# TensorE's column tiles take fourths of the tokens, and VectorE's block transposes lay attention output and sums into rows

## The chip, the cores and the metric

One core of one Trainium2 chip runs the whole program: TensorE (matmuls), VectorE, ScalarE, GpSimd, and SyncE (SP), which issues all DMAs. The metric is the device time of one execution in microseconds (us). Before the change it is 1421.83 us, the median of 3 runs (1418.3 to 1422.57).

## What is computed

Two conditioned attention layers on x (8 batches, 512 tokens, 512 channels). Layer 0 is linear attention with 8 heads; layer 1, the one that the change touches, is full softmax attention with 16 heads of 32 channels. Cut to what matters of layer 1:

```python
xn = layer_norm(x, norm_w, norm_b)
q = (xn @ q_w + q_b).reshape(8, 512, 16, 32)          # k alike
att = jnp.einsum('bnhl,bmhl->bnmh', q, k)             # + mask
att = jax.nn.softmax(att, axis=2)
v = ((xn @ v_w + v_b) * src_mask[:, :, None]).reshape(8, 512, 16, 32)
y = jnp.einsum('bnmh,bmhl->bnhl', att, v).reshape(8, 512, 512)
scale, shift = jnp.split((silu(emb) @ emb_w + emb_b)[:, None, :], 2, axis=2)
h = layer_norm(y, sb_norm_w, sb_norm_b) * (1.0 + scale) + shift
return x + silu(h) @ out_w + out_b
```

## The kernel before

Every float32 matrix product but two is made from rounded high parts and remainders, three matmuls a product (`product`, L508 to L510). Tokens come in four tiles of 128 (`NT`), channels in four of 128.

Layer 1's attention runs in 32 units n (`N1`), each one batch b and one group g of four heads, n = 4b + g. Of one unit, by steps of `the_order`:

- `qk`: queries and keys of two units ahead; SP stores them to DRAM (L1535, L1536) and loads them back as the stacks `Qs`, `Ks` (`stack`, L1548), once the current unit's `a` matmuls are done with the buffer.
- `S` (L665): scores of the next unit with tokens on partitions, 16 matmuls; VectorE takes each one's maximum (L1213). `nxt` (L673, L913) brings the negated maxima into rows of `Qs`.
- `a` (L682): the scores again, keys on partitions, with the maximum subtracted, 16 matmuls; ScalarE takes the exponential into `Pb` (L930).
- `pv` (L720), in two parts of two key tiles: values times exponentials into the bank PV. The four heads j of the group take the four column tiles of TensorE (32 output partitions each), and every product streams 512 tokens: PV is [head j and its 32 channels, 512 tokens].
- GpSimd adds the exponentials over the four key tiles (L1376; in the last unit VectorE too, L1242), and `den` (L698) sums them over partitions into the bank DEN with the selecting columns `sel`. It is queued ahead of the next unit's first `pv` part; after a batch's fourth unit it stands in `tlx`.
- `ae` (L938): ScalarE copies PV to `yt`; `tl`: TensorE makes four transposes of `yt` back into PV (helper `turn`, L503), ScalarE copies these to `yb` (L946), tokens on partitions; the semaphore `y1` then frees PV for the next unit.
- once a batch, `tlx`: ScalarE copies DEN to `yt` (L951), four transposes, VectorE takes the reciprocals `rd` (L1259), VectorE and GpSimd multiply `yb` (L1266, L1392). Then `ny` (layer norm, L1052 to L1060, L772), `ty` (transpose, scale, silu; GpSimd makes the remainder `sTl` and counts it in `s_lo`; its first step has SP load the residual rows into the four `wr`, L1497) and `o` (output product, L1199 and stores L1503), beside the units of the next batch.

The order on each engine is one list written out ahead: `weave` merges tracks of steps, and each track has start and end times in `PLAN`, as fractions of a unit (one entry for each g), between which its steps are spread by their `COST`. A unit's track may run past 1, and then ends the unit. Every engine, SP too, takes its own part of the list in order, and semaphores do the rest. PV and DEN are fixed banks; the other six go round.

Of the kernel before, what the change touches and what calls it, by code (L numbers as in the profile page):

```python
# [12 lines left out]
NT = T // 128  # L13
# [21 lines left out]
    "tl": (0.2, 0.1, 0.9), "tlx": (1.0, 0.0, 0.4, 0.4, 0.4, 0.4),  # L35
# [9 lines left out]
    "0q": ((0.109, 0.988), (0, 0.247), (0.978, 1.13)),  # L45
    "0o": ((0.012, 0.84), (0, 0.907), (0.06, 0.131)),
    "att": ((0.155, 0.254, 0.365, 0.543, 0.682), (0.002, 0.187, 0.345, 0.514, 0.66), (0.071, 0.271, 0.519, 0.672, 0.873), (0.001, 0.263, 0.332, 0.52, 0.685)),
    "pv": ((0.365, 0.753, 0.853), (0.337, 0.76, 0.879), (0.489, 1.021, 1.054), (0.328, 0.759, 0.832)),
    "tl": (None, (0, 0.931), (0, 0.654), (0, 0.723)),
    "tlx": ((0.007, 0.493), None, None, None),  # L50
    "ty": ((0, 0.666, 0.76), (0, 0.852, 0.94), (0, 0.862, 0.982), (0, 0.903, 1.096), (0, 0.953, 1.106)),
    "S": ((0.405, 0.476, 0.494, 0.654, 0.71), (0.151, 0.322, 0.491, 0.662, 0.834), (0.186, 0.267, 0.505, 0.626, 0.665), (0.211, 0.35, 0.409, 0.511, 0.65)),
    "nxt": ((0.847, 0.986), (0.899, 0.993), (0.866, 0.886), (0.724, 0.88)),
    "q": ((0.283, 0.391, 0.41), (0, 0, 0.02), (0, 0.151, 0.275), (0, 0.128, 0.394)),
    "k": ((0.337, 0.495, 0.596), (0, 0, 0.02), (0.187, 0.289, 0.357), (0.029, 0.298, 0.304)),
    "stack": ((0.802, 0.802), (0.489, 0.489), (0.812, 0.812), (0.683, 0.683)),
# [202 lines left out]
def cond_two_layers(nc, A, out):  # L259
# [4 lines left out]
    with ctx:  # L264
# [23 lines left out]
        yt = vt[1]  # L288
# [12 lines left out]
        rd = cU[:].rearrange("p a b -> p (a b)").rearrange("p (t g j) -> p t g j", t=NT, g=NG)  # L301
# [6 lines left out]
        sel = sb("sel", [128, 36])  # L308
# [37 lines left out]
        for i in range(2):  # L346
# [22 lines left out]
            "yT", "y1_tr", "y1", "den", "dT", "d1_tr", "rd", "y1_sc")}  # L369
# [124 lines left out]
        def _(e):  # L494
# [190 lines left out]
            def den(i, n):  # L685
                b, g = divmod(n, NG)
                pool, dve = ps_count(n, 3, 3)
                e.wait_ge(s["Ps_pool"], pool)
                if dve:
                    e.wait_ge(s["Ps_dve"], dve)  # L690
                if n == 0:
                    e.wait_ge(s["sel"], 2)
                    if bank_before["bank", 7] is not None:
                        e.wait_ge(*done(bank_before["bank", 7]))
                elif g == 0:
                    e.wait_ge(s["rd"], b)
                for j in range(4):
                    r = e.matmul(DEN[32 * j:32 * j + 32, :], sel[:, 4 - g:36 - g], p_buf(n, 0)[:, j, :],  # L698
                                 start=(g == 0), stop=(g == NG - 1))
                r.then_inc(s["den"], 1)  # L700

            def pv(i, n, first):

                b, g = divmod(n, NG)
                if first == 0 and g:
                    den(0, n - 1)
                for m in (first, first + 1):
                    e.wait_ge(s["P"], 16 * n + 4 * m + 4)
# [13 lines left out]
                    r.then_inc(s["PV"], 1)  # L722

            def tl(i, n):
                b, g = divmod(n, NG)
                if i == 1:
                    e.wait_ge(s["yT"], n + 1)
                    turn(PV, [yt[:, t * 128:(t + 1) * 128] for t in range(NT)]).then_inc(s["y1_tr"], 1)

            def tlx(i, b):  # L730
                if i == 1:
                    e.wait_ge(s["dT"], b + 1)
                    turn(DEN, [yt[:, t * 128:(t + 1) * 128] for t in range(NT)]).then_inc(s["d1_tr"], 1)

            parts = {"m": m, "mb": mb, "tx": tx, "k": k, "v": v, "te": te, "q": q, "st": state, "y": y, "ty": ty, "o": o,
                     "qk": qk, "S": S, "nxt": nxt, "a": a, "pv": pv, "den": den, "tl": tl, "tlx": tlx}
# [5 lines left out]
        def _(e):  # L742
# [189 lines left out]
            def ae(i, n):  # L932
                if n:
                    e.wait_ge(s["y1_tr"], n)
                if n and n % NG == 0:
                    e.wait_ge(s["d1_tr"], n // NG)
                e.wait_ge(s["PV"], 4 * n + 4)
                e.copy(yt[:], PV[:]).then_inc(s["yT"], 1)  # L938

            def tl(i, n):  # L940
                if i == 2:
                    b, g = divmod(n, NG)
                    if g == 0:
                        e.wait_ge(s["s_lo"], 4 * (8 + b))
                    e.wait_ge(s["y1_tr"], n + 1)
                    e.copy(yb[:, :, g * 128:(g + 1) * 128], t4(PV)).then_inc(s["y1"], 1)  # L946

            def tlx(i, b):
                if i == 0:
# [10 lines left out]
        def _(e):  # L960
# [290 lines left out]

            def tlx(i, b):
                if i == 1:
                    if b:
                        e.wait_ge(s["y1_sc"], 4 * b)
                    else:
                        e.wait_ge(s["y_sc"], 64)
                    e.wait_ge(s["d1_tr"], b + 1)
                    e.reciprocal(rd.rearrange("p t g j -> p t j g"),  # L1259
                                 DEN[:].rearrange("p (t j l) -> p t j l", t=NT, j=4)[:, :, :, 0:4]).then_inc(s["rd"], 1)  # L1260
                if i in (2, 4):
                    t = i - 2
# [3 lines left out]
                    e.tensor_tensor(y3, y3, rd[:, t, :, :].rearrange("p g j -> p (g j)").unsqueeze(2).to_broadcast([128, H1, 32]),  # L1266
                                    ALU.mult).then_inc(s["y1_sc"], 1)
# [3 lines left out]
                     "y": y, "ty": ty, "o": o, "qk": qk, "S": S, "nxt": nxt, "a": a, "ae": ae, "tlx": tlx}  # L1271
# [5 lines left out]
        def _(e):  # L1277
            def prologue():
# [10 lines left out]
                e.memset(sel[:, 4:5], 1.0).then_inc(s["sel"], 1)  # L1289
# [112 lines left out]
        def _(e):  # L1402
# [86 lines left out]
            def ty(i, x, c):  # L1489
                if i == 0 and c == 0:  # L1490
# [126 lines left out]
```

## Time and profile before

| | before |
|---|---|
| median of 3 runs | 1421.83 us |
| profiled execution | 1421.4 us |
| its span, first to last instruction | 1419.6 us |
| TensorE busy | 1345.7 us (95%) |
| VectorE busy | 1005.0 us (71%) |
| ScalarE busy | 821.8 us (58%) |
| GpSimd busy | 770.8 us (54%) |
| mean granted TensorE clock | 0.988 of full |

Layer 1's attention takes the span from about 545 us to 1385 us. In the rows, PE is TensorE's matmuls, PEld its weight loads, DVE VectorE, ACT ScalarE, POOL GpSimd, SPq the SP queue that issues DMAs. A matmul's duration is from its issue to its end, with the pipeline in it: matmuls that follow one another overlap. One float32 product with both operands unrounded shows as two matmuls. Some matmul records are missing from a trace.

### The profile page before, as it was taken

To read this page: it belongs to the slowest core of one execution; us is meant where nothing else is said; L and a number is where in the kernel's file an instruction comes from. 1 tells how busy PE (TensorE), PEld (TensorE's weight loads), DVE (VectorE), ACT (ScalarE), POOL (GpSimd) and SP (SyncE) were. 2 spreads that over 40 slices of the span, in tenths; PEclk is the share of its full clock that TensorE was granted. 3 is DMA by queue.
4 is the path that set the end of the run, shared out by engine and by line. 5 is a ranking of instruction groups with operands and counts; after the bars stand their busy time and mean duration, and the time that the engine had idled before them with its cause. 6 is when DMAs were issued, how large, how long until landed. Compare 5 with 4: busy or idle time off the path is not lost.

```text
span 1419.6 us, 20550 instructions
## 1 busy us (share of the span) xinstructions
PE 1345.7 (95%) x7040; PEld 971.0 (68%) x7040; DVE 1005.0 (71%) x1966; ACT 821.8 (58%) x1429; POOL 770.8 (54%) x692
## 2 busy tenths in 40 slices
PE   6899999999999899999999999999999999999887
PEld 4678888888888786566666665666666666666445
DVE  5788978778788876677657657657757756756645
ACT  4255455454554644756756756756756766666663
POOL 0323243332433515467657757757847847846863
PEclk9899999999999999999999999999999999999999
DMA  9021111311213275745545535534634634633602
GB/s 336 1 67 53 46 60 38 97 60 38 68 37 111 91 216 172 221 135 161 143 132 160 156 119 163 165 119 145 182 120 139 182 104 142 200 105 112 180 14 82
DMA packets 82888, 172.93 MB, mean 122 GB/s; under 512 B 7240, under 2 KB 7240, under 8 KB 82784
## 3 DMA queue, kind: packets, MB, share of 16 engines
q1 hardware_dynamic: 82784, 171.62, 39.3%
q8 instruction: 56, 0.92, 0.3%
q14 instruction: 48, 0.39, 0.1%
HBM read 104.45 MB, written 67.14 MB: 121 GB/s over the span
## 4 chain that ended last, share of the span: by engine, by line
PE 65%; DVE 14%; DMA 7%; ACT 6%; issue 3%; POOL 3%; SPq 1%; DVEq 0%; POOLq 0%; ACTq 0%
PE ps L508 13%; PE ps L510 12%; PE ps L509 12%; PE ps L665 6%; PE ps L720 6%; PE ps L682 6%; DVE cT L1213 5%; PE ps L503 4%; DMA Ks<-stack_scratch 4%; PE ps L698 2%; DVE st L1052 2%; POOL yb L1392 2%; PE ps L596 1%; PE ps L617 1%; ACT xTh L786 1%
## 5 line engine op out<-in xcount | busy, mean ns | idle before, releaser
L1376 POOL TENSOR_TENSOR Pb<-Pb 128x512 f32<-128x512 f32 x376 | 470.2, 1289 | 218.4 <-PE ps L720 218.2
L1213 DVE TENSOR_REDUCE cT<-ps 128x1 f32<-128x512 f32 x512 | 326.2, 685 | 131.1 <-PE ps L665 126.3
L930 ACT ACTIVATE Pb<-ps 128x512 f32<-128x512 f32 x512 | 285.9, 602 | 190.3 <-PE ps L682 184.2
L665 PE MATMUL ps<-Ks,Qs 98*128 98x512 f32 x512 | 194.9, 419 | 10.9 <-DMA Ks<-stack_scratch 8.3
L682 PE MATMUL ps<-Qs,Ks 106*128 106x512 f32 x512 | 199.2, 415 | 2.3 <-ACT Qs L913 1.4
L665 PEld LDWEIGHTS ps<-Ks,Qs 98*128 98x128 f32 x512 | 95.4, 191 | 70.9 <-DVE cT L1213 21.4
L682 PEld LDWEIGHTS ps<-Qs,Ks 106*128 106x128 f32 x512 | 95.2, 190 | 50.7 <-issue 25.4
L1299 POOL TENSOR_TENSOR rs<-ve,mhalf 128x4 f32<-128x4 f32 x32 | 33.0, 1032 | 167.8 <-DVE ve L1038 115.3
L1327 POOL TENSOR_TENSOR vt<-vt,qmx 128x512 f32<-128x512 f32 x32 | 33.7, 1055 | 166.1 <-DVE qmx L1130 166.1
L508 PE MATMUL ps<-xTh,Wh_k 128*128 128x512 f32 x256 | 106.5, 416 | 3.6 <-DVE xTl L1065 2.3
L508 PE MATMUL ps<-Wh_o,sTh 128*128 128x512 f32 x256 | 106.3, 415 | 0.2 <-DVE sTl L1191 0.2
L508 PE MATMUL ps<-Wh_v,xTh 128*128 128x512 f32 x256 | 102.9, 402 | 0.0
L510 PE MATMUL ps<-Wh_o,sTl 128*128 128x512 f32 x256 | 101.1, 395 | 0.0
L510 PE MATMUL ps<-Wh_v,xTl 128*128 128x512 f32 x256 | 100.7, 394 | 0.0
L510 PE MATMUL ps<-xTh,Wl_k 128*128 128x512 f32 x256 | 100.7, 393 | 0.0
L509 PE MATMUL ps<-Wl_o,sTh 128*128 128x512 f32 x256 | 100.6, 393 | 0.0
L509 PE MATMUL ps<-xTl,Wh_k 128*128 128x512 f32 x256 | 100.2, 391 | 0.0
L509 PE MATMUL ps<-Wl_v,xTh 128*128 128x512 f32 x256 | 100.2, 391 | 0.0
L1340 POOL TENSOR_TENSOR wr<-wr,boB 128x512 f32<-128x512 f32 x64 | 83.5, 1320 | 15.7 <-DMA wr<-in_x 13.7
L1199 DVE TENSOR_TENSOR wr<-ps,wr 128x512 f32<-128x512 f32 x64 | 43.8, 688 | 43.9 <-PE ps L510 31.8
L1113 DVE TENSOR_TENSOR ps<-ps,bvB 128x512 f32<-128x512 f32 x64 | 44.5, 697 | 40.5 <-PE ps L510 39.8
L1065 DVE TENSOR_TENSOR xTl<-ps,xTh 128x512 fp32r<-128x512 f32 x64 | 44.1, 688 | 39.6 <-ACT ps L788 39.2
(176 smaller groups left out, 2956.1 us busy)
## 6 DMA issues: line engine op xcount, KB each, us to landing
Qs<-stack_scratch SPq DMA_DIRECT2D x32, 768.0 KB
Ks<-stack_scratch SPq DMA_DIRECT2D x32, 768.0 KB
stack_scratch<-sg_q SPq DMA_DIRECT2D x32, 512.0 KB, 2.7
stack_scratch<-sg_k SPq DMA_DIRECT2D x32, 512.0 KB, 2.8
wr<-in_x SPq DMA_DIRECT2D x32, 256.0 KB, 4.8
x_scratch<-wr SPq DMA_DIRECT2D x32, 256.0 KB, 2.0
stack_scratch<-sg_q SPq DMA_DIRECT2D x32, 256.0 KB, 2.9
stack_scratch<-sg_k SPq DMA_DIRECT2D x32, 256.0 KB, 3.5
```

Of the source, the lines that this page charges most:

```text
L503: r = e.transpose(bank[:, t * 128:(t + 1) * 128], src, ident)
L508: e.matmul(bank[:], lh(k), rh(k), start=(k == 0), stop=False)
L509: e.matmul(bank[:], lh(k), rl(k), start=False, stop=False)
L510: return e.matmul(bank[:], ll(k), rh(k), start=False, stop=(k == NC - 1))
L665: e.matmul(bank[:], Qs[par][0:RX, j, t * 128:(t + 1) * 128], Ks[par][0:RX, j, :], start=True, stop=True).then_inc(s["S"], 1)
L682: e.matmul(bank[:], Ks[par][0:RE, j, m * 128:(m + 1) * 128], Qs[par][0:RE, j, :], start=True, stop=True).then_inc(s["ST"], 1)
L720: r = e.matmul(PV[32 * j:32 * j + 32, :], xbuf(8 + b)[:, m, h * 32:(h + 1) * 32], pb[:, j, :], start=(m == 0), stop=(m == NT - 1))
L930: e.activation(p_buf(n, m)[:, j, :], ps[bank_of["a", n, m, j]][:], ACT.Exp).then_inc(s["P"], 1)
L1113: e.tensor_tensor(ps[bank_of["v", x, t]][:], ps[bank_of["v", x, t]][:], bvB[:], ALU.add).then_inc(s["v_add"], 1)
L1213: e.tensor_reduce(nx[:, n % 2, j, t, 0:1], ps[bank_of["S", n, j, t]][:], AX.X, ALU.max, negate=True).then_inc(s["S_max"], 1)
L1340: e.tensor_tensor(wr[t][:], wr[t][:], boB[:], ALU.add).then_inc(s["xb"], 1)
L1376: e.tensor_tensor(acc[:, j, :], acc[:, j, :], p_buf(n, m)[:, j, :], ALU.add).then_inc(s["Ps_pool"], 1)
```

## The change

In `pv` and `den` a column tile no longer holds a head but a fourth u of the tokens: every product is cut in four along its tokens, 128 columns each, the four parts with the same weights go to the four column tiles, and the heads follow one another along the columns of the bank. PV becomes [fourth u and 32 channels, head j x 128 tokens], DEN [fourth u and 16 heads, 128 tokens]; `sel` is widened so that head h falls on row h. Then transposing every 32x32 block gives tokens on partitions at once. VectorE does so in one instruction for PV (`tl`) and one for DEN (`tlx`, into `dt`, a part of `vt[1]`); the two copies by ScalarE and the four transposes by TensorE go, for PV and for DEN. The partition of a token tile now holds tokens (u t r): 32 rows from each fourth, so the residual loads and the stores of layer 1 use `token_tile`. The transposition of PV waits for `s_lo` of that fourth of `yb` alone (4(7+b)+g+1); ScalarE's copy waited for all of the batch before, at g = 0. `PLAN` and two entries of `COST` are new.

```diff
-    "tl": (0.2, 0.1, 0.9), "tlx": (1.0, 0.0, 0.4, 0.4, 0.4, 0.4),
+    "tl": (0.3,), "tlx": (0.1, 0.3, 0.4, 0.4, 0.4, 0.4),
@@ PLAN, the entries that the prediction speaks of
-    "att": ((0.155, 0.254, 0.365, 0.543, 0.682), (0.002, 0.187, 0.345, 0.514, 0.66), (0.071, 0.271, 0.519, 0.672, 0.873), (0.001, 0.263, 0.332, 0.52, 0.685)),
-    "pv": ((0.365, 0.753, 0.853), (0.337, 0.76, 0.879), (0.489, 1.021, 1.054), (0.328, 0.759, 0.832)),
-    "tl": (None, (0, 0.931), (0, 0.654), (0, 0.723)),
-    "tlx": ((0.007, 0.493), None, None, None),
-    "ty": ((0, 0.666, 0.76), (0, 0.852, 0.94), (0, 0.862, 0.982), (0, 0.903, 1.096), (0, 0.953, 1.106)),
+    "att": ((0.155, 0.268, 0.393, 0.585, 0.737), (0.002, 0.187, 0.345, 0.514, 0.66), (0.071, 0.271, 0.519, 0.672, 0.873), (0.052, 0.275, 0.306, 0.477, 0.581)),
+    "pv": ((0.365, 0.753, 0.853), (0.337, 0.76, 0.879), (0.466, 1.021, 1.054), (0.328, 0.788, 1.044)),
+    "tl": (None, (0.073, 1.091), (0.073, 0.612), (0.102, 0.771)),
+    "tlx": ((0.007, 0.513), None, None, None),
+    "ty": ((0, 0.672, 0.766), (0, 0.858, 0.946), (0, 0.868, 0.988), (0, 0.965, 1.102), (1, 0.038, 0.099)),
-    "k": ((0.337, 0.495, 0.596), (0, 0, 0.02), (0.187, 0.289, 0.357), (0.029, 0.298, 0.304)),
-    "stack": ((0.802, 0.802), (0.489, 0.489), (0.812, 0.812), (0.683, 0.683)),
+    "k": ((0.351, 0.502, 0.539), (0, 0.02, 0.284), (0.13, 0.289, 0.341), (0.026, 0.264, 0.304)),
+    "stack": ((0.763, 0.763), (0.433, 0.433), (0.817, 0.817), (1.0, 1.0)),
@@ TensorE, den
                 elif g == 0:
-                    e.wait_ge(s["rd"], b)
+                    e.wait_ge(s["dT"], b)
                 for j in range(4):
-                    r = e.matmul(DEN[32 * j:32 * j + 32, :], sel[:, 4 - g:36 - g], p_buf(n, 0)[:, j, :],
-                                 start=(g == 0), stop=(g == NG - 1))
+                    h = 4 * g + j
+                    for u in range(4):
+                        r = e.matmul(DEN[32 * u:32 * u + 32, 0:128], sel[:, H1 - 1 - h:H1 + 31 - h],
+                                     p_buf(n, 0)[:, j, 128 * u:128 * u + 128], start=(h == 0), stop=(h == H1 - 1))
@@ TensorE, pv
-                        r = e.matmul(PV[32 * j:32 * j + 32, :], xbuf(8 + b)[:, m, h * 32:(h + 1) * 32], pb[:, j, :],
-                                     start=(m == 0), stop=(m == NT - 1))
+                        for u in range(4):
+                            r = e.matmul(PV[32 * u:32 * u + 32, 128 * j:128 * j + 128], xbuf(8 + b)[:, m, h * 32:(h + 1) * 32],
+                                         pb[:, j, 128 * u:128 * u + 128], start=(m == 0 and j == 0),
+                                         stop=(m == NT - 1 and j == 3))
@@ TensorE, tl and tlx: gone
-                    turn(PV, [yt[:, t * 128:(t + 1) * 128] for t in range(NT)]).then_inc(s["y1_tr"], 1)
-                    turn(DEN, [yt[:, t * 128:(t + 1) * 128] for t in range(NT)]).then_inc(s["d1_tr"], 1)
@@ ScalarE, ae, tl and tlx: gone
-                e.copy(yt[:], PV[:]).then_inc(s["yT"], 1)
-                    if g == 0:
-                        e.wait_ge(s["s_lo"], 4 * (8 + b))
-                    e.copy(yb[:, :, g * 128:(g + 1) * 128], t4(PV)).then_inc(s["y1"], 1)
-                    e.copy(yt[:], DEN[:]).then_inc(s["dT"], 1)
@@ VectorE
+            def tl(i, n):
+
+                b, g = divmod(n, NG)
+                e.wait_ge(s["s_lo"], 4 * (7 + b) + g + 1)
+                e.wait_ge(s["PV"], 4 * n + 4)
+                e.transpose(yb[:, :, g * 128:(g + 1) * 128].rearrange("p t (j d) -> p j t d", j=4),
+                            PV[:].rearrange("p (j t r) -> p j t r", j=4, t=NT)).then_inc(s["y1"], 1)
+
             def tlx(i, b):
+                if i == 0:
+                    if b:
+                        e.wait_ge(s["rd"], b)
+                    e.wait_ge(s["den"], 4 * b + 4)
+                    e.transpose(dt, DEN[:, 0:128]).then_inc(s["dT"], 1)
                 if i == 1:
...
-                    e.wait_ge(s["d1_tr"], b + 1)
-                    e.reciprocal(rd.rearrange("p t g j -> p t j g"),
-                                 DEN[:].rearrange("p (t j l) -> p t j l", t=NT, j=4)[:, :, :, 0:4]).then_inc(s["rd"], 1)
+                    e.wait_ge(s["dT"], b + 1)
+                    e.reciprocal(rd, dt.rearrange("p (t h) -> p t h", t=NT)[:, :, 0:H1]).then_inc(s["rd"], 1)
@@ SP
+            def token_tile(a, x, t):
+
+                if x < 8:
+                    return a[x, t * 128:(t + 1) * 128, :]
+                return a[x % 8].rearrange("(u t r) d -> t u r d", u=4, t=NT)[t]
...
-                        e.dma_start(wr[t][:], src[x % 8, t * 128:(t + 1) * 128, :]).then_inc(s[f"l_xr{t}"], 16)
+                        e.dma_start(wr[t][:], token_tile(src, x, t)).then_inc(s[f"l_xr{t}"], 16)
```

## Rows read from the trace of the kernel before

**Rows 1.** The page's busy time (us), share of the span, and instructions.

```profile
PE 1345.7 (95%) x7040; PEld 971.0 (68%) x7040; DVE 1005.0 (71%) x1966; ACT 821.8 (58%) x1429; POOL 770.8 (54%) x692
```

**Rows 2.** Windows: length; busy PE, PEld, DVE, ACT, POOL; granted clock, DMA share, GB/s.

```profile
640.00:1000.00 360.00, 349.99 (x1829) 231.09 (x1828) 239.87 (x431) 239.34 (x393) 254.08 (x210) 1.00 0.50 149
...
1331.00:1338.00 7.00, 7.00 (x38) 3.66 (x39) 3.46 (x5) 2.77 (x5) 2.31 (x3) 0.76 0.39 150
```

**Rows 3.** Waits in 640 to 1330 us: who waits for whom, total us, times, longest.

```profile
POOL Pb L1376 <- PE ps L720: 155.6, 25, 12.5
...
PEld ps L665 <- DVE cT L1213: 16.7, 46, 0.8
...
PE ps L665 <- DMA Ks<-stack_scratch: 5.2, 5, 1.6
```

**Rows 4.** Timeline, `den` and `pv`: start us, us, engine, line, what, count [idle before].

```profile
1007.42 0.40 PE L682 MATMUL ps<-Qs,Ks 106*128 106x512 f32 x1
...
1007.65 0.40 PE L665 MATMUL ps<-Ks,Qs 98*128 98x512 f32 x1
...
1007.98 1.07 PE L698 MATMUL ps<-Pb,sel 128*32 128x512 f32 x8
...
1008.86 1.90 PE L720 MATMUL ps<-Pb,xin 128*32 128x512 f32 x16
1008.87 0.13 PEld L720 LDWEIGHTS ps<-Pb,xin 128*32 128x32 f32 x4 [0.30 <-issue]
```

**Rows 5.** Timeline, weight loads of a `pv` part after a wait for ScalarE.

```profile
1376.32 0.16 PEld L720 LDWEIGHTS ps<-Pb,vf 128*32 128x32 f32 x8 [1.67 <-ACT Pb L930]
```

**Rows 6.** Timeline, a turn of `tl`; then the turns of `tlx` in two batches.

```profile
1003.85 0.47 PE L665 MATMUL ps<-Ks,Qs 98*128 98x512 f32 x1
...
1004.16 0.60 PE L503 MATMUL ps<-identr,vt 128*128 128x128 f32 x4
...
1004.52 0.47 PE L682 MATMUL ps<-Qs,Ks 106*128 106x512 f32 x1
...
1190.42 0.66 PE L503 MATMUL ps<-identr,vt 128*128 128x128 f32 x4 [0.38 <-ACT vt L951]
...
1299.44 0.65 PE L503 MATMUL ps<-identr,vt 128*128 128x128 f32 x4 [0.38 <-ACT vt L951]
```

**Rows 7.** Timeline around the start of a batch's second unit.

```profile
1316.52 2.48 SPq L1497 DMA_DIRECT2D wr<-x_scratch  x4
...
1319.52 0.48 SPq L1548 DMA_DIRECT2D Ks<-stack_scratch  x1
...
1326.99 0.86 PE L682 MATMUL ps<-Qs,Ks 106*128 106x512 f32 x3
...
1330.93 0.47 PE L665 MATMUL ps<-Ks,Qs 98*128 98x512 f32 x1 [3.08 <-DMA Ks<-stack_scratch]
```

**Rows 8.** Groups by form: count | busy us, mean ns of one | idle before.

```profile
L720 PE MATMUL ps<-Pb,xin 128*32 128x512 f32 x384 | 46.0, 596 | 0.0
L720 PEld LDWEIGHTS ps<-Pb,xin 128*32 128x32 f32 x384 | 10.9, 109 | 24.9 <-issue 22.6 <-ACT Pb L930 2.2
L938 ACT COPY vt<-ps 128x512 f32<-128x512 f32 x32 | 18.7, 585 | 23.9 <-PE ps L720 23.9
L503 PE MATMUL ps<-identr,vt 128*128 128x128 f32 x160 | 24.9, 278 | 4.1 <-ACT vt L951 3.4 <-ACT vt L938 0.8
L1065 DVE TENSOR_TENSOR xTl<-ps,xTh 128x512 fp32r<-128x512 f32 x64 | 44.1, 688 | 39.6 <-ACT ps L788 39.2
L1266 DVE TENSOR_TENSOR yb<-yb,cU 128x512 f32<-128x512 f32 x14 | 15.1, 1118 | 0.2
```

**Rows 9.** Timeline, the end after the last `pv`.

```profile
1385.43 1.07 PE L698 MATMUL ps<-Pb,sel 128*32 128x512 f32 x8 [0.96 <-DVE Pb L1242]
...
1386.55 0.59 ACT L951 COPY vt<-ps 128x512 f32<-128x512 f32 x1 [1.46 <-PE ps L698]
...
1387.95 0.56 DVE L1259 RECIPROCAL cU<-ps 128x64 f32<-128x64 f32 x1 [2.67 <-PE ps L503]
```

More of the change, by code:

```diff
@@ L287, in cond_two_layers @@
         wr = [sb(f"wr{i}", [128, D]) for i in range(4)]
-        yt = vt[1]
+        dt = vt[1][:, 0:128]
         bvB = sb("bvB", [128, D])
@@ L300, in cond_two_layers @@
         cU = sb("cU", [128, 8, B])
-        rd = cU[:].rearrange("p a b -> p (a b)").rearrange("p (t g j) -> p t g j", t=NT, g=NG)
+        rd = cU[:].rearrange("p a b -> p (a b)").rearrange("p (t h) -> p t h", t=NT)
         st = sb("st", [128, 2, NT, 6])
@@ L306, in cond_two_layers @@
         nm = sb("nm", [128, 2, NT])
-        sel = sb("sel", [128, 36])
+        sel = sb("sel", [128, 31 + H1])
         nx = cT[:].rearrange("p a b -> p (a b)").rearrange("p (n j t s) -> p n j t s", n=2, j=4, s=2)
@@ L368, in cond_two_layers @@
             "S", "S_max", "nx_set", "nx_hi", "nx_neg", "nx_lo", "nx_tr", "nxq", "ST", "P", "PV", "Ps_pool", "Ps_dve",
-            "yT", "y1_tr", "y1", "den", "dT", "d1_tr", "rd", "y1_sc")}
+            "y1", "den", "dT", "rd", "y1_sc")}
         def xbuf(x):
@@ L719, in pv @@
                         h = 4 * g + j
-                        r = e.matmul(PV[32 * j:32 * j + 32, :], xbuf(8 + b)[:, m, h * 32:(h + 1) * 32], pb[:, j, :],
-                                     start=(m == 0), stop=(m == NT - 1))
+                        for u in range(4):
+                            r = e.matmul(PV[32 * u:32 * u + 32, 128 * j:128 * j + 128], xbuf(8 + b)[:, m, h * 32:(h + 1) * 32],
+                                         pb[:, j, 128 * u:128 * u + 128], start=(m == 0 and j == 0),
+                                         stop=(m == NT - 1 and j == 3))
                     r.then_inc(s["PV"], 1)
[L724 to L727, printed above, removed]
-                    turn(PV, [yt[:, t * 128:(t + 1) * 128] for t in range(NT)]).then_inc(s["y1_tr"], 1)
-            def tlx(i, b):
-                if i == 1:
-                    e.wait_ge(s["dT"], b + 1)
-                    turn(DEN, [yt[:, t * 128:(t + 1) * 128] for t in range(NT)]).then_inc(s["d1_tr"], 1)
             parts = {"m": m, "mb": mb, "tx": tx, "k": k, "v": v, "te": te, "q": q, "st": state, "y": y, "ty": ty, "o": o,
-                     "qk": qk, "S": S, "nxt": nxt, "a": a, "pv": pv, "den": den, "tl": tl, "tlx": tlx}
+                     "qk": qk, "S": S, "nxt": nxt, "a": a, "pv": pv, "den": den}
             for p, i in order:
@@ L930, in a @@
                 e.activation(p_buf(n, m)[:, j, :], ps[bank_of["a", n, m, j]][:], ACT.Exp).then_inc(s["P"], 1)
[L932 to L937, printed above, removed]
-                e.copy(yt[:], PV[:]).then_inc(s["yT"], 1)
-            def tl(i, n):
-                if i == 2:
-                    b, g = divmod(n, NG)
-                    if g == 0:
-                        e.wait_ge(s["s_lo"], 4 * (8 + b))
-                    e.wait_ge(s["y1_tr"], n + 1)
-                    e.copy(yb[:, :, g * 128:(g + 1) * 128], t4(PV)).then_inc(s["y1"], 1)
-            def tlx(i, b):
-                if i == 0:
-                    e.wait_ge(s["den"], 4 * b + 4)
-                    e.copy(yt[:], DEN[:]).then_inc(s["dT"], 1)
             parts = {"w": w, "nx": nx_, "ny": ny, "tx": tx, "k": k, "te": te, "v": v, "q": q, "sta": sta, "y": y, "ty": ty,
-                     "early": early, "stacks": stacks, "qk": qk, "nxt": nxt, "a": a, "ae": ae, "tl": tl, "tlx": tlx}
+                     "early": early, "stacks": stacks, "qk": qk, "nxt": nxt, "a": a}
             for p, i in order:
@@ L1265, in tlx @@
                     y3 = yb[:, t, :].rearrange("p (h l) -> p h l", h=H1)
-                    e.tensor_tensor(y3, y3, rd[:, t, :, :].rearrange("p g j -> p (g j)").unsqueeze(2).to_broadcast([128, H1, 32]),
+                    e.tensor_tensor(y3, y3, rd[:, t, :].unsqueeze(2).to_broadcast([128, H1, 32]),
                                     ALU.mult).then_inc(s["y1_sc"], 1)
@@ L1270, in _ @@
             parts = {"early": early, "w": w, "mb": mb, "nx": nx_, "ny": ny, "tx": tx, "k": k, "te": te, "v": v, "q": q, "qn": qn, "sta": sta,
-                     "y": y, "ty": ty, "o": o, "qk": qk, "S": S, "nxt": nxt, "a": a, "ae": ae, "tlx": tlx}
+                     "y": y, "ty": ty, "o": o, "qk": qk, "S": S, "nxt": nxt, "a": a, "ae": ae, "tl": tl, "tlx": tlx}
             for p, i in order:
@@ L1288, in prologue @@
                 e.wait_ge(s["sel"], 1)
-                e.memset(sel[:, 4:5], 1.0).then_inc(s["sel"], 1)
+                e.memset(sel[:, H1 - 1:H1], 1.0).then_inc(s["sel"], 1)
                 e.wait_ge(s["sel"], 2)
@@ L1391, in tlx @@
                     y3 = yb[:, t, :].rearrange("p (h l) -> p h l", h=H1)
-                    e.tensor_tensor(y3, y3, rd[:, t, :, :].rearrange("p g j -> p (g j)").unsqueeze(2).to_broadcast([128, H1, 32]),
+                    e.tensor_tensor(y3, y3, rd[:, t, :].unsqueeze(2).to_broadcast([128, H1, 32]),
                                     ALU.mult).then_inc(s["y1_sc"], 1)
@@ L1502, in o @@
                     dst = x1d if x < 8 else out
-                    e.dma_start(dst[x % 8, t * 128:(t + 1) * 128, :], wr[t][:]).then_inc(s[f"st{t}"], 16)
+                    e.dma_start(token_tile(dst, x, t), wr[t][:]).then_inc(s[f"st{t}"], 16)
             def ahead(i):
```

8 lines of the change are left out of this document (4 added, 4 removed), and 14 rows, old and new, of the table PLAN.

## The prediction

> **What bounds the kernel now.** I read the busy table first: TensorE is busy 95% of the span, VectorE 71%, ScalarE 58%, GpSimd 54% [rows 1]. The averages mix two layers, so I took the stretch that the change touches, the second layer's attention: in 640 to 1000 us TensorE is busy 350.0 of 360 us, VectorE 239.9, ScalarE 239.3, GpSimd 254.1, at full granted clock [rows 2]. The waits of that stage say the same from the other side: GpSimd waits for TensorE's output products 155.6 us, while TensorE waits little for anybody: 16.7 us of weight loads held by VectorE's maxima, 5.2 us for the stacked keys [rows 3]. So a microsecond off TensorE's own stream is worth nearly a microsecond, and one off ScalarE or GpSimd nothing. The exception is one stall per batch, below.
>
> **TensorE's column tiles.** Before, the four heads of a group sit in the four column tiles and each product streams 512 tokens; one f32 product is two records (four products of `den` are 8 matmuls). A `pv` part of two key tiles is 16 records in 1.90 us [rows 4], mean 0.60 [rows 8], so four tiles go side by side and a group of four starts every (1.90 - 0.60)/3 = 0.43 us. After, a column tile takes 128 tokens: a group has a quarter of the columns, 0.43/4 = 0.11 us, and there are four times as many groups: per unit (one batch, four heads) 32 for `pv` and 8 for `den`, in 32 units 1280. If a group costs 0.11 us the array time is what it was: 32 x 0.11 + 8 x 0.11 = 4.3 us a unit against 10 x 0.43. The new cost is that four weight loads and four matmuls must be issued in each 0.11 us, one pair every 27 ns, where they now have 107 ns. The trace doesn't show this rate sustained. It shows two bounds. Lower: four weight loads, each 0.11 us long [rows 8], span only 0.13 us [rows 4], (0.13 - 0.11)/3 = 7 ns apart; even after a real wait for ScalarE eight weight loads begin and end in 0.16 us [rows 5]. That is a cost of nothing. Upper: full-array transposes of 128 columns start every (0.60 - 0.28)/3 = 0.107 us [rows 6, 8]; at this price for each pair a group costs 0.43 us, and 1280 x 0.32 = 410 us are added. The burst rows are the same instruction form in the same column tiles, while the transposes are explained by their 128 columns of weights and data, so I take nothing, and keep the middle for the range. Changes between 32-column tiles and the full array come as often as before, so they cost what they did.
>
> The row shows starts 7 ns apart in different column tiles. The Trainium skill (TensorEngine Tiling (Array Packing), Instruction Overhead) gives each matmul about 60 cycles of overhead, which for four tiles in turn would be an estimate of 0.10 us at the full clock, just inside the 0.11 us; the sum would be the same. A second figure of the skill (TensorE: Matmul & The Clock Gate, part 1) speaks against the change; it stands under the first rival.
>
> **What is removed from TensorE.** Each `tl` (PV transposed back by four transposes) goes. A scores matmul starts at 1003.85, the four transposes at 1004.16, the next matmul at 1004.52; the step from matmul to matmul is 0.67 us [rows 6], against 1007.65 - 1007.42 = 0.23 without a turn [rows 4]: 0.44 us each. In the stage there are 31 `tl` and 7 `tlx` turns: 38 x 0.44 = 16.7 us. Before each `tlx` turn TensorE also waits for ScalarE's copy, 0.38 us in the row [rows 6], 7 x 0.38 = 2.7 us: gone too, since TensorE waits for the sums' transposition only at the next batch's first `den`. Together 19.4 us.
>
> **What is given back.** Once a batch, in its second unit, TensorE stands still for the stacked keys: SP issued four loads of `wr` at 1316.52, then the keys' stack at 1319.52, and the score matmul that needs it ran at 1330.93 although the matmuls before it began at 1326.99 [rows 7]; three matmuls later (0.7 us) that is a stall of some 3.2 us, the longest of seven. The transfer doesn't get shorter if TensorE does, so one turn of each batch, which lies in the 11 us of the transfer, buys only a longer stall: 7 x 0.44 = 3.1 us. Left: 16.3 us.
>
> **The new order.** In the first unit of a batch it puts the key projection at 0.351 to 0.539 (was 0.337 to 0.596) and the stack at 0.763 (was 0.802). A unit takes 27 us (109.0 us from one batch's first turn to the next one's [rows 6], by four), so that is 1 to 1.5 us earlier. It also ends the unit's exponentials later (0.737, was 0.682), which the stack's wait on SP needs; `ty`'s first step with its four `wr` loads stays ahead of the stack on the same queue (0.672, was 0.666). Bounds: the stalls, 0.2 to 3.2 us each, may lose 1 us each, 7 us, or gain 1 us each. I take half the gain, 3 us.
>
> **ScalarE** loses two copies a unit and one a batch: 72 x 0.585 = 42 us of work [rows 8]. It isn't the bound; I cost it at nothing. Its copies also block the exponentials behind them in its queue, so this can only help.
>
> **VectorE** gets one 128x512 transposition a unit and a 128x128 one a batch. No row shows the operation. Nearest: 128x512 out of PSUM into SBUF 0.69 us; an upper bound is the product with a broadcast operand in two levels, 1.12 us [rows 8]. I take 0.69: 32 x 0.69 = 22 us over some 815 us, on an engine with a third of its time idle; on the path in the stage nothing. Behind the waiting transposition on VectorE are the maxima of scores, whose banks TensorE needs; but the transposition stands at 0.07 to 0.10 of the next unit, while the last `pv` part begins at 0.75 of its own and takes under 2 us, so the wait has ended. The other new wait, for one fourth of `yb` (`s_lo` at 4(7+b)+g+1), is weaker than the one for all of it that it replaces, and is on GpSimd's step of `ty`, which now lies later (0.965 to 1.102 and into the next unit); VectorE would wait there with the same maxima behind it. If the cover is gone in either way, the price is 32 x 0.69 = 22 us.
>
> No row here has the transposition; the Trainium skill (VectorE: DVE Perf Modes, The three transpose paths) has 311 ns for a bf16 128x128 in 32x32 blocks. An estimate by four of them is 1.24 us; the sum would be the same, since VectorE has the room, only the second rival would be dearer, by an estimated 18 us.
>
> **The end.** After the last `pv`: copy, transposes, copy, then `den` at 1385.43, released by VectorE's sums, copy 1386.55, transposes, reciprocal at 1387.95 [rows 9]. Of this `den` ends at 1386.50; a transposition by VectorE of perhaps 0.3 us and its hand-over put the reciprocal at 1386.9, and the first transposition of PV lies beside `den`. 1.1 us.
>
> **DMAs.** The residual rows are now four runs of 32 rows of 2 KB in place of 128 in a row. Packets stay 2 KB; SP's issue of four takes 2.48 us [rows 7]. Nothing to gain; at most the issue costs as much again, 28 x 0.6 = 17 us of SP, hidden unless it is ahead of the stack: 7 x 2.5 = 17 us. I take nothing.
>
> **Sum**: 16.3 + 3 + 1.1 = 20.4 us. The profiled execution took 1421.4 us (span 1419.6), the median of the runs is 1421.83, so no correction: 1421.4 - 20.4 = 1401 us.
>
> **Rivals.** (1) *The issue of TensorE becomes the bound of `pv` and `den`.* It decides from 27 ns a pair; each further nanosecond costs 1280 x 4 ns = 5.1 us. At 31 ns the gain is gone; halfway to the transposes, at 67 ns, 1280 x 4 x 40 ns = 205 us are added, 1606 us; at a mild 35 ns it is 41 us, 1442 us. For it: 64 pairs without a pause are nowhere in the trace. Against it: the bursts of rows 4 and 5. Chance 0.15. The Trainium skill (TensorE: Matmul & The Clock Gate, Part 1) gives, with one setting of the decoder, about 62 ns per matmul in the sequencer's ucode, which would be this rival.
> (2) *The change pays only in part*: what TensorE no longer does turns into longer waits for the stack, for the maxima, or for `y1`, which now comes out of VectorE's queue. With up to the 22 us of uncovered transpositions the result is 1410 to 1423 us; its middle 1416. For it: the stall of rows 7 is DMA time, and VectorE's maxima hold weight loads already. Against: these waits, 16.7 + 5.2 = 22 us in 690 [rows 3], are few. Chance 0.15.
> (3) *The order closes the stalls as well*: with half the longest as their mean they come to 7 x 1.6 = 11 us, 8 more than counted. It also removes the lower clock that followed the longest: in 1331 to 1338 us, full of matmuls, the granted clock is 0.76 [rows 2], (1 - 0.76) x 7 = 1.7 us. 1401 - 8 - 1.7 = 1391 us. For it: the stack is issued earlier. Against: the exponentials end later. Chance 0.12.
>
> **How the numbers follow.** Forecast 1401 us, 0.58; its own range 1395 to 1410. The range to hold 8 in 10 reaches over rivals 2 and 3 and the mild edge of rival 1: 1387 to 1425. A measurement of this kernel can tell about 0.3%, 4.3 us. Faster by more: the forecast, rival 3 and half of rival 2, 0.78; same: 0.08; slower: rival 1 but for its edge and the rest of rival 2, 0.14.
>
> **What would show it.** Right: groups of four 128-column matmuls start every 0.11 us, a `pv` part lasts 1.7 to 1.9 us; TensorE has no transposes of `vt`; VectorE's transposition takes 0.6 to 0.8 us; the four units of a batch take 109 - 2.5 us. Wrong: weight loads of `pv` farther apart than 27 ns with "issue" before them; VectorE idle behind TensorE's `pv` or GpSimd's `sTl` at the transposition; a stall before the second unit's scores that has grown by more than 1 us.

## The result: 1477.83 us, slower, where 1401 us was forecast

| | before | after |
|---|---|---|
| median | 1421.28 us (4 runs) | 1477.83 us (4 runs, 1473.6 to 1478.36) |
| ratio to before | | 1.0395, interval 1.0369 to 1.042 |
| profiled span | 1419.6 us | 1476.3 us |
| mean granted TensorE clock | 0.988 | 0.962 |

The page of the changed kernel: busy time by engine, beside [rows 1]:

```profile
PE 1350.6 (91%) x10720; PEld 1071.7 (73%) x10720; DVE 1033.1 (70%) x2006; ACT 785.4 (53%) x1357; POOL 771.4 (52%) x692
```

TensorE has 3680 records more and only 5 us more busy time. The stretch that answers to [rows 2] shows where time goes: the same 360 us hold less work on every engine (TensorE 350.0 before, VectorE 239.9, GpSimd 254.1).

```profile
640.00:1000.00 360.00, 332.30 (x3226) 259.06 (x3228) 234.54 (x420) 211.08 (x341) 236.66 (x195) 0.97 0.48 140
```

So all of them wait, and TensorE, the bound, is the one to ask. Its waits in the changed kernel, over the whole span (who waits for whom, total us, times, longest). The second line is the one that [rows 3] had at 5.2 us in the stage; over the whole span it was 8.3 us before:

```profile
PEld ps L665 <- issue: 62.5, 25, 9.3
PE ps L665 <- DMA Ks<-stack_scratch: 54.8, 8, 8.9
...
PEld ps L665 <- DVE cT L1185: 16.4, 50, 0.4
```

54.8 us in 8 waits for the load of the keys' stack: seven of 7.1 to 8.9 us, in the second unit of every batch but the first, and one of 1.1 us near the end. (Most of the "issue" time of the weight loads is the same time, seen in the other half of the engine: there the seven are 7.5 to 9.3 us. The expectations below count the stalls that way.) The waits of weight loads for VectorE's maxima, the last line, have not grown (21.4 us before). One stall for the keys' stack, the answer to [rows 7], as a timeline (start us, us, engine, line, what, count):

```profile
1124.05 3.03 SPq L1487 DMA_DIRECT2D wr<-x_scratch  x4
1127.18 2.62 SPq L1538 DMA_DIRECT2D Qs<-stack_scratch  x1
1129.85 2.57 SPq L1538 DMA_DIRECT2D Ks<-stack_scratch  x1
...
1137.34 0.39 PE L682 MATMUL ps<-Qs,Ks 106*128 106x512 f32 x1
...
1145.62 0.77 PE L665 MATMUL ps<-Ks,Qs 98*128 98x512 f32 x1 [7.89 <-DMA Ks<-stack_scratch]
```

SP issues the four loads of the residual, then the stack. An issue of the stack took 0.38 and 0.48 us before; here it takes 2.6 us, as if the queue were full (no row shows the queue itself). And the matmul that needs the keys runs 15.8 us after the issue began (before: 11.4 us). What the DMA engines do in this time stands in windows of the same stretch (length; busy PE, PEld, DVE, ACT, POOL; granted clock, DMA share, GB/s):

```profile
1124.00:1126.00 2.00, 2.00 (x30) 1.45 (x32) 2.00 (x4) 1.56 (x3) 2.00 (x3) 1.00 1.00 379
1126.00:1131.00 5.00, 4.55 (x74) 3.93 (x65) 4.69 (x10) 2.69 (x5) 5.00 (x6) 1.00 0.38 92
1131.00:1138.00 7.00, 6.73 (x30) 5.05 (x28) 4.92 (x9) 6.12 (x11) 6.33 (x6) 1.00 0.96 240
1138.00:1140.00 2.00, 0.00 (x0) 0.00 (x0) 0.22 (x2) 0.43 (x1) 1.31 (x2) 1.00 0.90 354
1140.00:1145.00 5.00, 0.00 (x0) 0.00 (x0) 0.00 (x0) 0.00 (x0) 2.43 (x2) 0.66 0.26 94
1145.50:1152.00 6.50, 6.38 (x15) 4.79 (x15) 3.31 (x6) 2.37 (x4) 0.00 (x0) 0.51 0.04 17
```

In 1140 to 1145 us, where TensorE waits, the DMA engines are busy to 26% and move 94 GB/s. A full stretch is 379 GB/s. A quarter of 16 engines is 4, and the new pattern of the residual has a leading dimension of 4 (fourths u), with 32 rows each. The last line is the second price: after 8 us without a matmul the granted clock is at its lower level, 0.51, through 6.5 us of dense matmuls. It fell during the wait already (0.66 in 1140 to 1145 us).

**Theory A**: a DMA whose leading dimension has four entries is carried by four of the 16 engines; the residual's 1 MB lies there for some 10 us, and the stack's load, queued behind it, is complete only when its share on these four engines is. **Theory B**: the new order (PLAN) holds up the stack. **Theory C**, the first rival of the prediction: TensorE's issue. The trace alone decides C. Groups and timeline of the changed kernel:

```profile
L723 PE MATMUL ps<-Pb,vf 128*32 128x128 f32 x2048 | 64.5, 279 | 2.9 <-ACT Pb L923 2.9
L700 PE MATMUL ps<-Pb,sel 128*32 128x128 f32 x1024 | 35.9, 283 | 1.1 <-DVE Pb L1214 1.1
```

```profile
1046.35 1.69 PEld L723 LDWEIGHTS ps<-Pb,xin 128*32 128x32 f32 x64 [0.37 <-issue]
1046.35 1.95 PE L723 MATMUL ps<-Pb,xin 128*32 128x128 f32 x64
```

64 matmuls in 1.95 us, 16 groups, one every (1.95 - 0.28)/15 = 0.11 us, as the same work took 1.90 us in [rows 4]. C is out.

### The profile page after: what moved, and what is told of

The parts are those of the page before. It is cut to its first block, busy times and chain, and to the rows that moved or that the text cites. A ratio compares the mean times of both kernels' runs of the same rounds, so it can differ in the third digit from the quotient of the medians.

```text
span 1476.3 us, 27878 instructions
## 1 busy us (share of the span) xinstructions
PE 1350.6 (91%) x10720; PEld 1071.7 (73%) x10720; DVE 1033.1 (70%) x2006; ACT 785.4 (53%) x1357; POOL 771.4 (52%) x692
## 4 chain that ended last, share of the span: by engine, by line
PE 63%; DVE 12%; DMA 12%; ACT 6%; SPq 3%; issue 2%; POOL 1%; POOLq 0%; DVEq 0%; ACTq 0%
PE ps L508 12%; PE ps L510 11%; PE ps L509 11%; DMA Ks<-stack_scratch 8%; PE ps L665 7%; PE ps L682 7%; PE ps L723 6%; DVE cT L1185 5%; PE ps L503 3%; PE ps L700 2%; ACT Qs L906 2%; ACT ps L781 1%; ACT xTh L779 1%; PE ps L596 1%; SPq L1487 1%
## 5 line engine op out<-in xcount | busy, mean ns | idle before, releaser
L665 PE MATMUL ps<-Ks,Qs 98*128 98x512 f32 x512 | 198.9, 430 | 58.7 <-DMA Ks<-stack_scratch 54.8
L665 PEld LDWEIGHTS ps<-Ks,Qs 98*128 98x128 f32 x512 | 99.6, 197 | 103.5 <-issue 62.5
L682 PEld LDWEIGHTS ps<-Qs,Ks 106*128 106x128 f32 x512 | 99.8, 197 | 50.0 <-issue 14.1
L510 PE MATMUL ps<-Wh_o,sTl 128*128 128x512 f32 x256 | 104.3, 407 | 0.0
L509 PE MATMUL ps<-Wl_o,sTh 128*128 128x512 f32 x256 | 103.8, 406 | 0.0
L906 ACT CAST Qs<-ps 10x1024 fp32r<-10x1024 f32 x64 | 61.3, 1003 | 21.8 <-PE ps L673 20.6
```

What stands on the lines that cost most here:

```text
L509: e.matmul(bank[:], lh(k), rl(k), start=False, stop=False)
L510: return e.matmul(bank[:], ll(k), rh(k), start=False, stop=(k == NC - 1))
L665: e.matmul(bank[:], Qs[par][0:RX, j, t * 128:(t + 1) * 128], Ks[par][0:RX, j, :], start=True, stop=True).then_inc(s["S"], 1)
L682: e.matmul(bank[:], Ks[par][0:RE, j, m * 128:(m + 1) * 128], Qs[par][0:RE, j, :], start=True, stop=True).then_inc(s["ST"], 1)
L906: e.copy(Qs[n % 2][RM:RE, 2 * h:2 * h + 2, :], rows).then_inc(s["nxq"], 1)
```

## The experiments

Each run is compared with runs of the kernel before on the same chip. The last column is the total of TensorE's waits for the keys' stack over the whole span of the profiled execution; it was 8.3 us before the change and 54.8 us after it.

| run | median us | before us | ratio, interval | waits for the keys' stack, us |
|---|---|---|---|---|
| e1 rows as before | 1405.67 | 1421.01 | 0.9886, 0.9852 to 0.992 | 9.8 |
| e2 loads as before | 1410.57 | 1421.01 | 0.9918, 0.9893 to 0.9943 | 7.7 |
| e3 stores as before | 1470.43 | 1421.01 | 1.0341, 1.0297 to 1.0385 | 56.6 |
| e4 before, with blocks | 1497.96 | 1421.01 | 1.0536, 1.0508 to 1.0564 | 61.4 |
| e5 eight blocks | 1445.75 | 1420.63 | 1.0172, 1.0148 to 1.0197 | 30.6 |
| e6 sixteen blocks | 1407.60 | 1420.63 | 0.9903, 0.9881 to 0.9925 | 9.7 |
| e7 fourths leading by 32 rows | 1413.47 | 1420.63 | 0.9944, 0.9924 to 0.9965 | 11.3 |
| e8 e1 with the old order | 1429.42 | 1420.63 | 1.0064, 1.0039 to 1.0089 | 14.9 |
| e9 before, with the new order | 1443.63 | 1422.66 | 1.0172, 1.0125 to 1.0218 | 4.2 |
| e10 e7, loads early | 1399.43 | 1422.66 | 0.9853, 0.9818 to 0.9889 | 1.1 |
| e11 after, loads early | 1407.75 | 1422.66 | 0.9909, 0.9875 to 0.9943 | 1.0 |
| e12 before, loads early | 1411.39 | 1422.66 | 0.9926, 0.9901 to 0.9951 | none |

**Undo the pattern of the DMAs: both, loads alone, stores alone.**

```diff
 # e1, in token_tile
-                return a[x % 8].rearrange("(u t r) d -> t u r d", u=4, t=NT)[t]
+                return a[x % 8, t * 128:(t + 1) * 128, :]
 # e2, the loads alone
-                        e.dma_start(wr[t][:], token_tile(src, x, t)).then_inc(s[f"l_xr{t}"], 16)
+                        e.dma_start(wr[t][:], src[x % 8, t * 128:(t + 1) * 128, :]).then_inc(s[f"l_xr{t}"], 16)
 # e3, the stores alone
-                    e.dma_start(token_tile(dst, x, t), wr[t][:]).then_inc(s[f"st{t}"], 16)
+                    e.dma_start(dst[x % 8, t * 128:(t + 1) * 128, :], wr[t][:]).then_inc(s[f"st{t}"], 16)
```

> The changed kernel, but layer 1's residual loads and stores take 128 rows in a row, as before the change; the residual then belongs to other tokens, the amount of work is the same. Theory A (a DMA whose leading dimension is four blocks of 32 rows is carried by 4 of the 16 engines; the stack's load queues behind it): the seven stalls of 7.4 to 9.3 us fall to under 2 us, the low clock after them goes, 1400 to 1408 us. Theory B (the new order is what delays the stack): the stalls stay, 1465 to 1480 us.

> The changed kernel, but only the residual loads take 128 rows in a row (the residual then belongs to other tokens); the stores stay in four blocks. Theory A, with the loads ahead of the stack as the cause: at most 5 us above the run with both undone, 1402 to 1412 us. If the stores hold the stack's engines too: 1430 us or more.

> The changed kernel, but only the stores of layer 1 take 128 rows in a row (so rows of the output change places); the loads stay in four blocks. Theory A with the loads as the cause: the stalls stay within 1 us, 1465 to 1480 us. If the stores matter as much: 1440 us or less.

1405.67, 1410.57 and 1470.43 us: each time is in the range of A with the loads as the cause. Of e1's signs one didn't come fully: two of its stalls are 2.0 and 2.5 us, and behind these the granted clock is still low (0.72 in 1318.32 to 1324.32 us). The pattern of the residual costs 1477.8 - 1405.7 = 72 us, and its loads carry nearly all of it. With the loads alone as before 5 us are left, and the intervals of e1 and e2 overlap; with the stores alone as before 65 us are left.

Where the time went is seen best in TensorE's busy time, 1350.6 us in the changed kernel and less in e1:

```profile
PE 1338.8 (95%) x10720; PEld 1064.0 (75%) x10720; DVE 1031.6 (73%) x2006; ACT 785.1 (56%) x1357; POOL 772.0 (55%) x692
```

The two profiled spans are 1476.3 - 1409.8 = 66.5 us apart (e1's profiled execution was the slowest of its four). The waits for the stack account for 54.8 - 9.8 = 45 us. The same matmuls are busy 12 us longer, and the lower clock accounts for it: summed over windows of 2 us, the clock lost while TensorE was busy comes to an estimated 34 us in the one and 22 us in the other. The remaining 10 us are idle time of TensorE that no run took apart. The mean granted clock, 0.962 and 0.981, would suggest (1 - 0.962) x 1476 = 56 us against (1 - 0.981) x 1410 = 27 us, 29 us apart; but part of that low clock lies inside the waits, where no matmul runs, so it can't be added to the 45 us.

**The pattern alone, in the kernel before.** The diff is the reverse of e2 and e3 on that kernel.

> The kernel before with one part of the change alone: residual loads and stores in four blocks of 32 rows (the residual then belongs to other tokens). Theory A: stalls of 7 to 10 us for the keys' stack in each batch's second unit and low clock behind them, 1475 to 1500 us. Theory B: within 5 us of before.

1497.96 us, 77 us more, with seven stalls of 8.1 to 9.5 us. The cost needs neither the new tiles nor VectorE's transposition nor the new order, and B is out as the cause of the long stalls.

**One size changed: eight and sixteen blocks.**

```diff
-                return a[x % 8].rearrange("(u t r) d -> t u r d", u=4, t=NT)[t]
+                return a[x % 8].rearrange("(u t r) d -> t u r d", u=8, t=NT)[t]      # e6: u=16
```

> The changed kernel, with residual rows in eight blocks of 16 rows in place of four of 32 (the residual then belongs to other tokens). Theory A (as many DMA engines carry such a transfer as it has blocks): 8 of 16 engines, stalls of some 2 to 4 us, 1415 to 1445 us. If any transfer in blocks is slow: as the changed kernel, 1465 to 1485 us.

> The same with sixteen blocks of 8 rows. Theory A: all 16 engines, within 5 us of the run with rows as before: 1401 to 1411 us. If the blocks as such cost: over 1420 us.

1445.75 us (0.75 us above the range's upper end) and 1407.60 us. The stalls of e5 are 2.7 to 6.6 us, longer than the expected 2 to 4. How the transfers go is read best in the last batch, where SP issues stores and loads of the residual and no stack: the changed kernel, e5 and e6.

```profile
1446.00:1454.00 8.00, 6.64 (x20) 4.69 (x19) 7.53 (x19) 7.46 (x20) 0.00 (x0) 0.50 0.27 98
```

```profile
1422.00:1428.00 6.00, 3.56 (x11) 2.49 (x12) 5.73 (x15) 5.75 (x16) 0.79 (x1) 0.80 0.53 173
```

```profile
1384.00:1388.00 4.00, 1.45 (x10) 0.75 (x8) 3.57 (x9) 3.75 (x11) 1.16 (x1) 1.00 1.00 278
```

Shares of 0.27, 0.53 and 1.00 with leading dimensions of 4, 8 and 16 are what A says. The rates are 98, 173 and 278 GB/s. And since sixteen blocks cost no more than rows in a row (ratios 0.9903 and 0.9886, their intervals overlap), no cost of blocks as such is seen. The Trainium skill (DMA: Bandwidth & Descriptors, Rules for kernel authors) states it: the number of engines of a DMA is set by the slowest dimension of its access patterns that isn't of size 1, and fewer than 16 entries confine it to at most as many. These windows agree.

**A residual that keeps the right tokens and all 16 engines.**

```diff
-        wr = [sb(f"wr{i}", [128, D]) for i in range(4)]
+        wrs = sb("wr", [128, 4, D])
+        wr = [wrs[:, i, :] for i in range(4)]
+            def fourth(a, x, u):
+
+                return a[x % 8, 128 * u:128 * u + 128, :].rearrange("(t r) d -> r t d", t=NT)
 # ty, SP: load u in place of load t; GpSimd waits for all four before the first
+                            e.dma_start(wrs[32 * t:32 * t + 32, :, :], fourth(src, x, t)).then_inc(s[f"l_xr{t}"], 16)
 # o, SP: batches 8 to 14, once the last product is added
+                            for u in range(4):
+                                e.dma_start(fourth(out, x, u), wrs[32 * u:32 * u + 32, :, :]).then_inc(s[f"st{u}"], 16)
```

> The changed kernel, whole and with the right tokens; the residual of layer 1 is loaded and stored one fourth u at a time into one tile of 128x4x512, 32 partitions leading, four DMAs a batch as before; the stores wait for the batch's last output product, but for the last batch, which stores each tile in four parts. Theory A: 32 leading rows reach all 16 engines, no long stall, 1400 to 1412 us. If the late stores or the loads' completion together cost: 1415 to 1430 us.

1413.47 us: 0.56% under the kernel before, but 8 us above e1; it lies between the two forecasts. Its waits for the stack are still 0.8 to 3.1 us each, 11.3 us in all. That is 1.5 us more than in e1, so they don't explain the 8 us, which no run took apart.

**The order: old order with the new tiles, new order with the old tiles.** e8 is e1 with the old PLAN, e9 the kernel before with the new one. `tl` is three steps in the kernel before and one in the changed kernel, so in both runs the times of PLAN meet a list of steps that they were not made for.

> The changed kernel with rows as before and with the order (PLAN) of the kernel before; the residual belongs to other tokens. The forecast's sum gave the order 3 us: 1405 to 1413 us. If the new order carries the gain: 1418 us or more. If the order costs: 1400 us or less.

> The kernel before with one part of the change alone, the new order (PLAN). If the order is worth its 24 us by itself (the run with the old order minus the one with the new): 1395 to 1405 us. If it is worth it only together with the removed turns and copies, whose places it closes: within 8 us of before, 1413 to 1430 us.

1429.42 us is above what the forecast's 3 us for the order would give and falls under "the new order carries the gain"; 1443.63 us is outside both ranges. The four corners, with contiguous residual rows:

| | old order | new order |
|---|---|---|
| old tiles, ScalarE's copies, TensorE's turns | 1421 | 1443.6 |
| new tiles, VectorE's transposition | 1429.4 | 1405.7 |

Each half alone loses, 8.8 and 21 us; together they gain 15. Waits of e8 in 640 to 1320 us:

```profile
ACT yb L765 <- POOL nm L1286: 28.9, 7, 4.5
PEld ps L665 <- ACT Pb L923: 18.7, 18, 2.4
ACT Pb L923 <- POOL Pb L1360: 17.2, 8, 2.6
PE ps L665 <- ACT Pb L923: 11.6, 7, 2.0
```

In the kernel before, ScalarE's layer norm of `yb` has no such wait. In one batch, as a timeline of e8:

```profile
1097.67 0.81 ACT L765 ACTIVATE yb<-yb,nm,rs 128x512 f32<-128x512 f32 x1 [4.09 <-POOL nm L1286]
...
1099.60 0.81 PE L665 MATMUL ps<-Ks,Qs 98*128 98x512 f32 x2 [1.62 <-ACT Pb L923]
```

With two copies and a turn fewer, the old times put ScalarE's layer norm (`ny`) at a place where its scale isn't ready. ScalarE stands 4.1 us in front of it, with exponentials queued behind, and TensorE waits for them. In e1 the same wait of ScalarE is 6.4 us in all. In e9 the new times ask for TensorE's turn before ScalarE's copy is done, weight loads of `pv` wait longer for the exponentials (4.9 us before), and the layer norm waits here too (640 to 1320 us again):

```profile
PEld ps L720 <- ACT Pb L930: 25.4, 55, 1.0
ACT yb L772 <- POOL nm L1302: 20.3, 6, 3.4
...
PEld ps L503 <- ACT vt L938: 12.5, 7, 1.8
PE ps L503 <- ACT vt L938: 11.5, 7, 1.6
```

Which of these waits carries how much of the 24 us between e8 and e1 was not tried singly; the account by these waits is argued, not shown.

**Loads early.** The 1 MB of the residual is issued at the start of the batch's first unit, when the stack's load isn't due, in place of its two thirds.

```diff
+            def tlx(i, b):
+                if i == 0 and b < 7:
+                    residual(8 + b)
             def ty(i, x, c):
-                if i == 0 and c == 0:
+                if i == 0 and c == 0 and (x < 8 or x == 15):
+                    residual(x)
```

> The whole change with the residual moved by fourths, and its loads issued at the start of the batch's first unit in place of its two thirds, so that they are no longer queued ahead of the stack (the last batch's stay). Theory A' (what is left of the stall is the residual's 1 MB in front of the stack): the stalls of 1.6 to 3.5 us shrink below 1 us, 1403 to 1410 us. If they come from the stack's own 1.5 MB: 1410 to 1416 us.

> The changed kernel with its loads in four blocks of 32 rows left as they are, but issued at the start of the batch's first unit. Theory A (the harm is only that the stack queues behind four slow engines): the loads take their 10 us beside other work, 1408 to 1425 us. If four engines held that long delay the other transfers too (the keys and queries to DRAM, the next x): 1440 us or more.

> The kernel before, with its contiguous loads issued at the start of the batch's first unit. Its stalls for the stack were 1.3 to 3.5 us: Theory A' 1410 to 1418 us; if they come from the stack's own transfer: within 4 us of before.

1399.43, 1407.75 and 1411.39 us. e10 is the whole change and 3.6 us under the expected range; of the waits for the stack one of 1.1 us is left, near the end, and in the stretch of [rows 2] TensorE is busy 352.4 us (350.0 before the change). e11 is 0.25 us under its range, e12 in the range of A'. The page of e10 and its window:

```profile
PE 1330.4 (95%) x10720; PEld 1057.9 (76%) x10720; DVE 1032.5 (74%) x2006; ACT 784.1 (56%) x1357; POOL 771.2 (55%) x692
```

```profile
640.00:1000.00 360.00, 352.36 (x3431) 273.73 (x3432) 258.64 (x464) 229.75 (x373) 260.35 (x215) 1.00 0.54 155
```

e11 keeps the changed kernel's slow loads, only sooner: its timeline has SP issuing them for 8.65 us at a place where no engine waits for a DMA. In e10, with loads by fourths at the same place, the four issues take 2.10 us:

```profile
1166.85 0.39 SPq L1389 DMA_DIRECT2D vf<-x_scratch  x1
1167.30 8.65 SPq L1495 DMA_DIRECT2D wr<-x_scratch  x4
```

```profile
1167.41 2.10 SPq L1504 DMA_DIRECT2D wr<-x_scratch  x4
```

e11 is 70 us faster than the changed kernel and 8 us slower than e10, which loads and stores the residual by fourths. So nearly all of the harm is the place of the slow loads ahead of the stack on the same queue; some 8 us are left that four engines in themselves may cost. e12 shows that the kernel before had the same stall in small: the early loads are worth 11 us there, and 14 us from e7 to e10. Best kernel against best kernel, 1399.43 against 1411.39 us: 12 us, 0.8%, is what the tiles, VectorE's transposition and the order are worth together, with the residual by fourths.

## Why the prediction was wrong, point by point

- *What bounds the kernel.* Right: TensorE's stream. Each engine lost work in the stage when TensorE stood.
- *Column tiles, 1280 groups at 0.11 us.* Right: 0.11 us a group, 64 pairs in a row. The bursts of [rows 4, 5] were the nearer rows. The cost is small and not quite nothing: the matmuls of `pv` and `den` are busy 158.5 us in the kernel before and 163.1 us in e1, part of it at a lower clock. Rival 1 (0.15) did not happen: a pair of weight load and matmul took 27 ns, not 62.
- *TensorE's removed turns, 19.4 us.* The work did go: TensorE is busy 1345.7 us before, 1338.8 in e1 and 1341.0 in e8. But the sum took it as gained wherever it lay. In e8, with the turns gone and the old order, TensorE is idle 1432.2 - 1341.0 = 91 us where it was idle 74 before, and the kernel loses 8.8 us: with an order written out by hand, what is queued behind a removed step comes sooner at its next wait.
- *The new order, 3 us.* A term that was mis-sized: 1429.42 - 1405.67 = 24 us with the new tiles, and 21 us lost with the old. The entries were compared one by one with the same stall in view; their fit to the new step lengths was not.
- *What is given back, 3.1 us.* The right place, and the wrong size. The stall at the keys' stack was named, as DMA time in which less TensorE work is no gain. The waits grew from 8.3 to 54.8 us in all. The prediction's sign, a stall before the second unit's scores grown by more than 1 us, came true in all seven batches, for a reason that the prediction didn't have.
- *DMAs: nothing, at most 17 us of issue.* This is the step that failed, and it decided the result. It priced the issue on SP and the size of the packets, and took the transfer's own time as unchanged. The loads went to four of the 16 engines, and undoing that alone (e2) takes the kernel from 1477.83 to 1410.57 us, 67 us. The upper bound should have been a transfer four times as long in front of the stack, in every batch. The Trainium skill's rule quoted above (DMA: Bandwidth & Descriptors, Rules for kernel authors) would have given it; the prediction's line on DMAs doesn't use it.
- *VectorE.* Right: one 128x512 transposition of 32x32 blocks takes 0.71 us (0.69 was taken), the 128x128 one 0.32 us, and VectorE's wait for `pv` in front of it is 11.6 us in all, while TensorE's waits for the maxima behind it did not grow. The figure of the Trainium skill (VectorE: DVE Perf Modes, The three transpose paths), 311 ns for bf16 128x128, gave times four an estimate of 1.24 us; the measurement decides.

```profile
L1229 DVE STREAM_TRANSPOSE yb<-ps 128x512 f32<-128x512 f32 x32 | 22.7, 708 | 11.6 <-PE ps L723 11.6
L1237 DVE STREAM_TRANSPOSE vt<-ps 128x128 f32<-128x128 f32 x8 | 2.5, 316 | 2.5 <-PE ps L700 1.6
```

- *ScalarE.* It lost 821.8 - 785.4 = 36 us of work, where 42 were taken, and that is worth nothing, as forecast. "This can only help" was wrong: in e8 ScalarE comes too early at its layer norm and holds the exponentials behind it.
- *The end, 1.1 us.* Nothing of it is seen. From the last `den` ([rows 9]) to the first transposition of `yb` it is 12.98 us before and 12.93 us in e10. But in e10 this `den` lies at the lower clock (0.50 in 1361 to 1363 us) and takes 1.94 in place of 1.07 us; at the full clock the step would be an estimated 0.9 us shorter. First the kernel before, then e10:

```profile
1398.41 1.50 PE L503 MATMUL ps<-identr,yb 128*128 128x128 f32 x12 [2.37 <-POOL yb L1320]
```

```profile
1360.99 1.94 PE L701 MATMUL ps<-Pb,sel 128*32 128x128 f32 x32 [1.77 <-DVE Pb L1215]
...
1373.92 1.50 PE L504 MATMUL ps<-identr,yb 128*128 128x128 f32 x12 [1.37 <-POOL yb L1305]
```

- *The sum.* With the DMA step taken out (e1) the kernel takes 1405.67 us, 5 us from the forecast. That is partly luck: it holds two terms that were wrong in opposite directions, 16.3 us for turns that with the old order cost 8.8 us, and 3 us for an order worth 24.
- *The rivals.* The side that came was none of them. Rival 2 came nearest, with longer waits for the stack, but priced them by TensorE's freed time, not by the transfer. "Slower" had 0.14, all of it for other reasons.

## What to carry to other kernels

Read every changed access pattern of a DMA for its leading dimension, and price the transfer itself with so many of 16 engines, then ask what is queued behind it: the cost lands on the next load that somebody waits for. A step taken out of an order written by hand is not a saving until the order is made for the new lengths; test the change and its order as a pair, since here each alone is slower. And a stall that is already in the trace before is where a slower transfer will show first; moving 1 MB out of its way was worth 11 and 14 us, as much as the change.

## What the runs showed of the hardware that was not expected

- DMAs of 256 KB with a leading dimension of 4, 8 or 16 kept the DMA engines busy to 0.27, 0.53 and 1.00, at 98, 173 and 278 GB/s.
- With the loads on four engines in the queue, SP's next issue took 2.6 us in place of 0.4, and where a 1 MB load stood before them, the four issues took 8.65 us in place of 2.10: slow transfers hold up the issuing engine too.
- In the 6 us of dense matmuls behind each of the seven long stalls the granted clock was 0.50 to 0.74. TensorE's busy time was 12 us longer than in e1, beside the 45 us of waiting.
- In column tiles of 32 columns, f32 weight load and matmul pairs ran at one per 27 ns, 64 pairs in a row: 1.95 us where pairs four times as long took 1.90.
- VectorE transposed 128x512 f32 in 32x32 blocks, from PSUM to SBUF, in 0.71 us, and 128x128 in 0.32 us.
